# Shared-key attention in half-array tiles with a null column, and a new opening order in the delta rule

## The reference

```
h  = layernorm(x)
q  = h @ Wq                      (16 heads of 64)
kv = h @ Wkv                     (64, keys and values at once)
s  = q . kv / 8, causal;  s_null = q . null / 8
p  = softmax over [s_null, s]
o  = p_null * null + sum_j p_j * kv_j
x += concat(o) @ Wout
```

## Time and profile before

| | us |
|---|---|
| median of 3 runs | 1533.64 (1533.50 to 1539.13) |
| profiled execution | 1534.92 |
| its span | 1533.1 |
| granted TensorE clock, mean | 0.871 |
| first attention, first projection to last add to x | 18.0 to 153.1 |
| opening of the delta rule, first projection to first product of keys | 586.0 to 641.35 |

### The profile page before, as it was taken

How to read it: one execution, slowest core, us unless ns; L and a number is a source line. 1 busy time by engine, 2 the same in 40 slices (tenths; PEclk the granted TensorE clock), 3 DMA queues, 4 the chain that set the end, 5 groups by cost and what they waited for, 6 DMA issues and landing times. The chain is left out here.

```text
span 1533.1 us, 24885 instructions
## 1 busy us (share of the span) xinstructions
PE 1239.6 (81%) x9007; PEld 811.6 (53%) x9008; DVE 892.1 (58%) x2157; ACT 716.1 (47%) x1292; POOL 324.3 (21%) x349
## 2 busy tenths in 40 slices
PE   6999896358697996577776874779789989797998
PEld 3788464237465663235644651765544444364776
DVE  3787473766676546586677568446643455474211
ACT  2444463341274324386568454436566633364432
POOL 0222200003211003454447351021000034300000
PEclk9999798566798997796987897689889999698999
DMA  7000000020000000000000000016045900000000
GB/s 269 1 0 0 1 2 1 0 85 1 1 2 1 1 0 1 0 1 2 1 1 1 1 1 0 2 46 262 2 106 117 211 13 1 0 2 2 1 0 15
DMA packets 15200, 44.28 MB, mean 29 GB/s; under 512 B 1872, under 2 KB 4976, under 8 KB 14448
## 3 DMA queue, kind: packets, MB, share of 16 engines
q1 hardware_dynamic: 15088, 42.80, 9.4%
HBM read 42.01 MB, written 0.79 MB: 28 GB/s over the span
## 5 line engine op out<-in xcount | busy, mean ns | idle before, releaser
L725 DVE TENSOR_REDUCE L_xattn_top<-banks 128x4 f32<-128x512 f32 x128 | 80.7, 672 | 43.9 <-PE banks L585 43.8
L730 DVE TENSOR_TENSOR L_xattn_p<-banks,L_xattn_top 128x512 f32<-128x512 f32 x128 | 82.5, 686 | 4.8
L682 ACT ACTIVATE L_xattn_p<-L_xattn_p 128x512 f32<-128x512 f32 x128 | 75.8, 630 | 18.3 <-DVE L_xattn_p L730 18.2
L690 ACT ACTIVATE L_xattn_pT<-banks 128x512 f32<-128x512 f32 x128 | 69.7, 595 | 19.7 <-PE banks L598 19.7
L585 PE MATMUL banks<-L_xattn_ks,L_xattn_qT 32*128 32x512 f32 x256 | 74.7, 671 | 1.6 <-ACT L_xattn_qT L671 1.6
L598 PE MATMUL banks<-w_const,L_xattn_p 128*128 128x128 f32 x512 | 69.5, 278 | 6.4 <-ACT L_xattn_p L682 6.4
L1252 DVE TENSOR_TENSOR L_ffn_a<-L_ffn_a,L_ffn_share 128x512 f32<-128x512 f32 x64 | 39.9, 686 | 57.6 <-DMA L_ffn_share<-L_ffn_shares 37.0
L1166 PE MATMUL banks<-L_ffn_a,region_a 128*128 128x512 f32 x136 | 67.4, 600 | 4.9 <-DVE L_ffn_a L1252 4.9
L1485 ACT ACTIVATE L_ffn_aT<-banks,L_ffn_shift 128x512 f32<-128x512 f32 x64 | 43.3, 687 | 58.9 <-PE banks L1437 57.3
L1498 DVE SCALAR_TENSOR_TENSOR x<-banks,L_ffn_combine,x 128x128 f32<-128x128 f32 x64 | 18.0, 345 | 88.7 <-PE banks L1448 88.7
L1157 PE MATMUL banks<-hT,region_a 128*128 128x512 f32 x136 | 68.5, 609 | 0.0
(11 more groups left out here) (515 smaller groups left out, 3131.2 us busy)
## 6 DMA issues: line engine op xcount, KB each, us to landing
L_ffn_share<-L_ffn_shares SPq DMA_DIRECT2D x32, 512.0 KB, 9.5
region_b<-in_L_ffn SPq DMA_DIRECT2D x1, 6216.0 KB, 28.9
region_a<-in_L_ffn SPq DMA_DIRECT2D x1, 4416.0 KB, 13.5
region_b<-in_L_attn SPq DMA_DIRECT2D x1, 3150.5 KB, 11.7
region_a<-in_L_ffn SPq DMA_DIRECT2D x1, 3080.5 KB, 21.2
region_b<-in_L_attn SPq DMA_DIRECT2D x1, 1633.5 KB, 9.1
region_b<-in_L_xattn SPq DMA_DIRECT2D x1, 835.0 KB, 9.8
w_tables<-in_tables SPq DMA_DIRECT2D x1, 832.0 KB, 12.8
```

Source lines behind the costliest of these rows:

```text
L682: nc.scalar.activation(p[:, m % 4, :], p[:, m % 4, :], ACT.Exp, scale=scale).then_inc(exped, 1)
L690: nc.scalar.activation(pT[:, n % 2, 2 * (P % 2) + e, :], tps[e][:], ACT.Copy).then_inc(pT_kept, 1)
L725: nc.vector.tensor_reduce(top[:, i, :], rows_of(score[i][:], 4), X, ALU.max)
L730: nc.vector.tensor_tensor(rows_of(p[:, i, :], 4), rows_of(score[i][:], 4), bc(top[:, i, :], 2, T), ALU.subtract).then_inc(centered, 1)
```

## The change

The layer norm of the first attention moves into its block (`NORM_INSIDE`), and the two blocks become one, with the first two units between the projections. Everything is written out, with no loop of the sequencers. The queries stay in two halves of 64 partitions and the keys are held twice, in the upper and the lower half: two heads are scored by products of 64 rows in either half of the array, into two banks. The null key is column 129 of the keys, so a unit's scores are 129 wide (130 with padding), the maximum, the exponential and the sum take it along, and no step of its own is left for it. The exponential reads PSUM and takes the maximum as a bias; its sums come out of the same instruction. GpSimd scales the weights before they are turned. The values have the null vector subtracted, and null @ Wout, the same for every token, is added to x once, at the start. Mixing has the values as weights and gives the outputs already transposed, two heads to the upper and two to the lower half of PSUM, copied by VectorE; the projection follows for two units at once. The copies of the turned weights go to ScalarE and VectorE by turns.

In the delta rule three tiles are projected ahead of `make_rates` and the last ones ahead of the norms of the queries; the two tiles of keys come first; GpSimd takes the taps of tile 2 (values) in place of tile 1, and raises the key norms ahead of squaring the queries' tiles.

```diff
--- before.py
+++ after.py
@@ the old multi_query_attention goes as a whole; a new one stands behind class Norm @@
+def multi_query_attention(nc, g, w, st):
+    NH, DH, Q = 16, 64, 4
+    UNITS = B * NH // Q
+    SCALE = DH ** -0.5
+    W = T + 2
+    norm = Norm(nc, g, st)
+    qT, kvT, kv = st.sb("qT", [128, NH // 2, TOK]), st.sb("kvT", [128, B, W]), st.sb("kv", [T, B, DH])
+    causal, null_wide = st.sb("causal", [T, W], BF16), st.sb("null_wide", [128, T])
+    top, shift, sums, inv = (st.sb(s, [T, 4, Q]) for s in ("top", "shift", "sums", "inv"))
+    p, pT, oT = st.sb("p", [T, 4, Q, W]), st.sb("pT", [T, 3, Q * T]), st.sb("oT", [128, 4, 2 * T])
...
+    tps, oT_bank, out_bank = bank[6], bank[7][:, 0:2 * T], bank[7][:, 2 * T:3 * T]
...
+            nc.gpsimd.memset(causal[:, T:W], 0.0)
+            nc.gpsimd.tensor_copy(causal[:, 0:T], g.causal_bf[:, 0, :]).then_inc(null_ready, 1)
+            pool.wait_ge(w.loaded, 16)
+            nc.gpsimd.tensor_tensor(kvT[:, :, T], bc(w["null2"][:, 0], 1, B), bc(w["null2"][:, 1], 1, B), ALU.add)
+            nc.gpsimd.tensor_tensor(kvT[:, :, T + 1], bc(w["null2"][:, 0], 1, B), bc(w["null2"][:, 1], 1, B), ALU.add)
+            nc.gpsimd.tensor_tensor(null_wide[:], bc(w["null2"][:, 0], 1, T), bc(w["null2"][:, 1], 1, T),
+                                    ALU.add).then_inc(null_ready, 1)
+            norm.invert(pool, 0)
+            norm.invert(pool, 1)
+            for m in range(UNITS):
+                pool.wait_ge(inverted, m + 1)
+                nc.gpsimd.tensor_tensor(p[:, m % 4, :, 0:T], p[:, m % 4, :, 0:T], bc(inv[:, m % 4, :], 2, T),
+                                        ALU.mult).then_inc(normed, 1)
...
+            def make(i, lhsT, half):
+                if i >= 4:
+                    await_kept(pe, i - 4)
+                nc.tensor.matmul(part(i)[:], lhsT, g.hT[:, half * HALF:(half + 1) * HALF], start=True, stop=True).then_inc(made, 1)
...
+                if s >= 3:
+                    pe.wait_ge(exped, s - 2)
+                for a in range(2):
+                    nc.tensor.matmul(bank[k + a][:, 0:2 * W], g.ident_bf[:], bc(causal[:], 1, 2), start=True, stop=False,
+                                     skip_group_check=True)
+                for j in range(2):
+                    for a in range(2):
+                        last = nc.tensor.matmul(bank[k + a][:, j * W:(j + 1) * W],
+                                                qT[64 * a:64 * a + 64, 2 * q + j, n * T:(n + 1) * T],
+                                                kvT[64 * a:64 * a + 64, n, :], start=False, stop=True,
+                                                skip_group_check=True)
+                last.then_inc(scored, 1)
+            def turn(m):
+                pe.wait_ge(normed, m + 1)
+                if m >= 1:
+                    await_pT(pe, m - 1)
+                for i in range(Q):
+                    last = nc.tensor.transpose(tps[:, i * T:(i + 1) * T], p[:, m % 4, i, 0:T], g.ident)
+                last.then_inc(turned, 1)
+            def mix(m):
+                await_pT(pe, m)
+                if m >= 1:
+                    pe.wait_ge(oT_kept, m)
+                if m >= 3:
+                    pe.wait_ge(added, (m - 1) // 2)
+                for a in range(2):
+                    last = nc.tensor.matmul(oT_bank[64 * a:64 * a + 64, :], kv[:, m // 4, :],
+                                            pT[:, m % 3, 2 * a * T:2 * (a + 1) * T], start=True, stop=True)
+                last.then_inc(mixed, 1)
+            def project(h):
+                pe.wait_ge(oT_kept, min(2 * h + 3, UNITS))
+                if h >= 1:
+                    pe.wait_ge(added, h)
+                for m in (2 * h, 2 * h + 1):
+                    for j in range(2):
+                        pair = 2 * (m % 4) + j
+                        last = nc.tensor.matmul(out_bank, oT[:, m % 4, j * T:(j + 1) * T],
+                                                w["wout"][:, pair * D:(pair + 1) * D],
+                                                start=(m % 2 == 0 and j == 0), stop=(m % 2 == 1 and j == 1))
+                last.then_inc(projected, 1)
+            pe.wait_ge(w.loaded, 16)
+            pe.wait_ge(null_ready, 2)
+            for j in range(NH // 2):
+                last = nc.tensor.matmul(bank[0][:, 0:D], null_wide[:], w["wout"][:, j * D:(j + 1) * D],
+                                        start=(j == 0), stop=(j == NH // 2 - 1))
+            last.then_inc(null_done, 1)
+            norm.turn(pe, 0, part(0))
+            pe.wait_ge(kept_act, 1)
+            make(KV0, w["wkv2"], 0)
+            make_queries(Q0[0])
+            norm.turn(pe, 1, part(3))
+            make_queries(Q0[1])
+            make_queries(Q0[2])
+            make_queries(Q0[3])
+            make_values(VAL0, 0)
+            scores(0)
+            make_queries(Q0[4])
+            make_queries(Q0[5])
+            make_queries(Q0[6])
+            scores(1)
+            make_queries(Q0[7])
+            make(KV1, w["wkv2"], 1)
+            for i in Q1:
+                make_queries(i)
+            make_values(VAL1, 1)
+            for s in range(2, UNITS + 6):
+                if s % 2 == 1 and 0 <= s - 7:
+                    project((s - 7) // 2)
+                if s < UNITS:
+                    scores(s)
+                if 0 <= s - 4 < UNITS:
+                    mix(s - 4)
+                if s - 2 < UNITS:
+                    turn(s - 2)
+            def weigh(s):
+                act.wait_ge(shifted, s + 1)
+                if s >= 4:
+                    act.wait_ge(turned, s - 3)
+                k = 2 * (s % 3)
+                for a in range(2):
+                    for j in range(2):
+                        i = 2 * a + j
+                        last = nc.scalar.activation(p[:, s % 4, i, 0:T + 1], bank[k + a][:, j * W:j * W + T + 1], ACT.Exp,
+                                                    bias=shift[:, s % 4, i:i + 1], scale=SCALE,
+                                                    accum_out=sums[:, s % 4, i:i + 1])
+                last.then_inc(exped, 1)
...
+            for s in range(2, UNITS + 2):
+                if s < UNITS:
+                    weigh(s)
+                if s % 2 == 0:
+                    keep_turned(s - 2)
...
+            def keep_values(i, half):
+                dve.wait_ge(made, MADE.index(i) + 1)
+                nc.vector.tensor_tensor(kv[:, 4 * half:4 * half + 4, :], rows_of(part(i)[:, 0:4 * DH], 4),
+                                        bc(w["null_row"][:, 0:DH], 1, 4), ALU.subtract).then_inc(kept_dve, 1)
...
+            def find_shift(s):
+                dve.wait_ge(scored, s + 1)
+                nc.vector.tensor_reduce(top[:, s % 4, :].rearrange("p (a j) -> p a j", a=2), both_banks(s), X, ALU.max)
+                dve.drain()
+                nc.vector.tensor_scalar(shift[:, s % 4, :], top[:, s % 4, :], -SCALE, None, ALU.mult).then_inc(shifted, 1)
+            def invert(m):
+                dve.wait_ge(exped, m + 1)
+                nc.vector.reciprocal(inv[:, m % 4, :], sums[:, m % 4, :]).then_inc(inverted, 1)
...
+            for s in range(2, UNITS + 6):
+                if s % 2 == 1 and 0 <= s - 7:
+                    add((s - 7) // 2)
+                if s % 2 == 0 and 0 <= s - 3 < UNITS:
+                    keep_turned(s - 3)
+                if s < UNITS:
+                    find_shift(s)
+                if 2 <= s - 1 < UNITS:
+                    invert(s - 1)
+                if 0 <= s - 4 < UNITS:
+                    keep_mixed(s - 4)
@@ -2355,10 +2439,10 @@
     NH, DK, DV, TAPS, G, NB = 12, 64, 128, 4, 4, 32
     GROUPS = NH // G
     ORDER = (2, 3, 0, 1, 4, 5, 6, 7)
-    FIRST = (2, 4, 3, 0, 1, 5, 6, 7)
+    FIRST = (2, 3, 4, 0, 1, 5, 6, 7)
     bank, banks = g.bank, g.banks
     TILES = [M for M in range(8 * GROUPS) if M < 8 or M % 8 < 4]
-    pool_tiles = [M for M in TILES if (M == 1 or M >= 8)]
+    pool_tiles = [M for M in TILES if (M == 2 or M >= 8)]
     dve_tiles = [M for M in TILES if M not in pool_tiles]
 
     rate, beta, e, u1, log_u, fix = (st.sb(x, [T, B, NH]) for x in ("rate", "beta", "e", "u1", "log_u", "fix"))
@@ -2536,12 +2620,12 @@
             for i in range(4):
                 last = nc.gpsimd.tensor_copy(pick[:, i, 2 * i:2 * i + 2], g.const["half"])
             last.then_inc(pick_set, 1)
-            add_taps(1)
+            add_taps(2)
             square_tile(0, first_squares(0))
-            square_tile(2, first_squares(1))
-            square_tile(3, first_squares(2))
+            square_tile(1, first_squares(1))
             for part in range(4):
                 key_norms(0, part)
+            square_tile(3, first_squares(2))
             square_tile(4, first_squares(3))
             for hg in range(GROUPS):
                 first, more = B * hg, hg + 1 < GROUPS
@@ -2760,19 +2844,19 @@
             pe.wait_ge(w.loaded, 16)
             project(0)
             project(1)
+            project(2)
```

(39 more changed lines are left out.)

332 lines of the change are left out of this document (128 added, 204 removed).

## The result

The changed kernel takes 1512.07 us (median of 4 runs, 1510.89 to 1513.18), where the kernel before took 1534.45 on the same chip (4 runs, 1533.5 to 1539.13). The ratio is 0.9846, 95% interval 0.9823 to 0.9869: 22.4 us less, where the prediction said 28. The profiled execution of after took 1513.18 us with a span of 1511.4; TensorE's mean granted clock over the span is 0.872, and 0.871 before, so the mean clock isn't behind the gain.

A forecast was written before the change was run, and what follows sets the result against it. A ring between VectorE and TensorE was taken to bound the first attention. Gains of 24 us there and 4 in the delta rule, 28 off 1533.6, gave 1505.6 us; range for 8 in 10: 1493 to 1516.

The forecast's parts named there:

- The ring: First attention: VectorE and TensorE wait on each other in turn, 5.7 us for two units, 2.85 a unit.
- TensorE's own sum: First attention: TensorE's work alone, 2.4 us a unit, or 2.75 if the mixing is serial, against 3.08 before.
- The tenth for a change of form: First attention, TensorE: each switch from one form of tile to another costs 0.1 us, about 0.2 a unit.
- Rival (a): First attention: ring not closed, TensorE bounds at 2.4 us a unit, 1494 us; with dear switches 1509; chance 0.22.
- The first projection: Start of the attention stage: first projection at about 18.2 us, no gain on 18.00 before.
- units 3 to 6: First attention: these units have no projection yet and follow the ScalarE ring, 2.3 us each.
- The tail: End of the attention stage: the last unit falls through the chain in 7.8 us, last addition at 129 us.
- The delta rule: Delta rule's opening: taps out of the way, GpSimd's powers end last, first key matmul at 637.2 for 641.3; gain 4 us.
- rival (e): Delta rule gains nothing because the powers take the place of the taps: +4, 1510 us; inside the forecast's range, no separate chance.
- (c): First attention: tiles of 64 do not run side by side in mixing or scores; 1516 us; chance 0.06.
- (d): First attention: TensorE idles and its clock falls; gain gone from 14 of 32 units, 1568 us with all; chance 0.04.
- (b): First attention: ScalarE's exponentials with sums are dear, 3.0 to 3.2 us a unit, 1513 us; chance 0.15.

The follow-up runs named there:

- the copy on ScalarE: The changed kernel with the copy of the mixed outputs moved from VectorE to ScalarE, TensorE's order untouched: 1511.95 us, ratio 0.9847 to the kernel before.
- the attention-alone run: The changed kernel with the old delta rule put back: 1521.93 us, ratio 0.9880 to the kernel before.
- the delta rule alone: The kernel before with only the new delta rule, its attention as before: 1537.16 us, ratio 0.9991 to the kernel before.
- without sums: The changed kernel with no running sums in the exponentials, the sums set to 1: 1517.22 us, ratio 0.9883 to the kernel before.
- the masks first: The changed kernel with the masks ahead of the projection in TensorE's odd steps: 1510.54 us, ratio 0.9827 to the kernel before.
- the squares first: The changed kernel with GpSimd's two last squarings ahead of its four powers in the delta rule's opening: 1514.98 us, ratio 0.9846 to the kernel before.

## Why the prediction was right, and where it was off

**The ring.** It was right in place, order and size: 5.5 us a pair against 5.7. Its proof is the copy on ScalarE. TensorE's own sum was forecast at 2.4 us a unit and is 2.565: masks to scores 0.31, scores to mixing 0.65, mixing to turning 0.58, turning to masks 0.49, projection 0.53. The tenth for a change of form that was taken from the earlier trace rows fits the masks (two products of 0.11 and 0.1 make 0.31) and falls short at the scores (0.55 forecast, 0.65 measured). Rival (a) named the right second bound with a wrong price: opening the ring gives 5 us in the stage, not 11.

The Trainium skill (TensorEngine Tiling (Array Packing), PSUM Bottleneck) advises both ScalarE and VectorE for emptying PSUM; here moving one of VectorE's two copies gave 0.4 us a pair, so the trace agrees.

**The terms that were mis-sized**, all in the attention, 24 us forecast and 18.8 measured (153.1 to 134.3). The first projection came 1.2 late, because loads ended later in this execution: that of the context, as the first row shows beside the earlier trace rows, and that of the weights, which took 10.8 us where the earlier trace rows has 9.1. GpSimd's operations on the null vector, which read these weights, released the second row.

```profile
9.27 1.94 PE L178 MATMUL banks<-w_const,context_ctx 128*128 128x128 f32 x8 [9.27 <-DMA context_ctx<-in_ctx]
14.12 3.75 PE L409 MATMUL banks<-region_b,L_attn_null_wide 128*128 128x128 f32 x16 [2.92 <-POOL L_attn_null_wide L322]
```

```profile
region_b<-in_L_attn SPq DMA_DIRECT2D x1, 1633.5 KB, 10.8
```

Then 0.6 up to the third unit, and 1.3 in units 3 to 6, 10.3 us for 9. The 25 units after gave 1.2 back (69.8 us for 71). The tail took 11.4 for 7.8, and this 3.6 is the largest miss: I walked one unit through the chain and left out the rounds of earlier units that share bank 7 and VectorE's order with it; banks of their own gave back 2.0 of it. 1.2 + 0.6 + 1.3 - 1.2 + 3.6 = 5.5, the difference to 24 but for rounding.

Only the last two terms are the same in another trace of this attention, that of the attention-alone run. There the first projection starts at 17.9 us, its first four instructions take 1.98 us where after's took 3.76, units 3 to 6 take 9.3, and the last addition ends at 130.1, 1.1 us behind the forecast and not 5.3. So 4.2 us of the attention's miss differ from one execution to the next, with the landing of the loads and TensorE's pace at the start and in units 3 to 6, and a hit or a miss of that size is partly luck.

**The delta rule.** The taps are out of the way and GpSimd's powers, with the squares behind them, come last, as forecast; TensorE's norm products wait for them. After has

```profile
606.08 3.94 DVE L3086 SCALAR_TENSOR_TENSOR region_a<-banks,region_b,region_a 128x1000 f32<-128x1000 f32 x3
```

```profile
606.17 6.45 POOL L2588 TENSOR_TENSOR L_attn_rk<-L_attn_rk,L_attn_power 128x8 f32<-128x8 f32 x4 [10.90 <-DVE L_attn_rk L3117]
612.59 3.74 POOL L2583 TENSOR_TENSOR L_attn_PT<-region_a 128x1024 f32<-128x1024 f32 x2
```

```profile
614.62 1.08 PE L2698 MATMUL banks<-L_attn_PT,L_attn_pick 128*32 128x256 f32 x8 [14.11 <-POOL L_attn_PT L2583]
```

Beside the trace of before that is 5.3 us in the opening and 3.7 in the stage, for a forecast of 4. Beside the old order's other trace it is 1.3 and 0.2, and the timed runs of the delta rule alone hold 0 and 4 us alike. So the order of events was right, but rival (e), no gain, isn't refuted, and that 3.7 lies so near the 4 may be luck. The landmark was badly chosen, too: key matmul and coefficients fell together before, and only the second carries the stage.

**The other rivals.** (c) is out: products on 64 rows or columns run in pairs. (d) is out: the granted clock is 0.98 from 48 to 120 us. (b) is out but for units 3 to 6, where the sums cost 0.7 us in all; the tail without sums took 11.0 us for 11.4.

## What to carry to other kernels

Where two engines hand a pair of steps to and fro, take one instruction off the engine that is not busy and see whether the busy one speeds up: that tells a ring from a full engine, which a reordering on the full one does not, since it changes that engine's own work too. Don't take missing idle time for a wait that is gone: look how closely the instruction follows the one that releases it (0.05 us here, in after and with the masks first). Count the tail of a pipeline bank by bank, with every round that shares one. Choose the landmark whose distance to the stage's end stays nearly constant while the clock does. And set a stage beside more than one trace of the same code before a gain of a few us in it is believed.

## What was not expected of the hardware

Some small operations of VectorE take as long as the squaring that GpSimd is at. Here is the same instruction in after, with GpSimd idle, and in the run with the squares first, where GpSimd squares from 590.9 to 599.1:

```profile
595.41 0.26 DVE L2168 TENSOR_TENSOR L_attn_u<-L_attn_u,L_attn_fix 128x96 f32<-128x96 f32 x1
```

```profile
594.75 1.83 DVE L2168 TENSOR_TENSOR L_attn_u<-L_attn_u,L_attn_fix 128x96 f32<-128x96 f32 x1
...
597.49 1.74 DVE L2172 TENSOR_TENSOR L_attn_e<-L_attn_e,L_attn_log_u 128x96 f32<-128x96 f32 x1
```

Two such cost the earlier squares 3 us of their gain. The Trainium skill (SBUF — State Buffer, SBUF: two separate sides) has VectorE with two inputs in SBUF wait for a whole instruction of GpSimd at a port they share; the 1.8 us beside GpSimd's 1.87 agree.

Each exponential with a sum is two instructions, and the second adds 0.09 us to the pace (0.34 for one in after, 0.25 without sums):

```profile
65.43 0.36 ACT L459 ACTIVATE L_attn_p<-banks,L_attn_shift 128x129 f32<-128x129 f32 x1
65.68 0.20 ACT L459 ACTIVATION_READ_ACCUMULATOR L_attn_p<-banks,L_attn_shift 128x1 f32 x1
```

And the stages behind the first attention, with the same code, took 1376 to 1382 us together in the traces with the new delta rule as it stands in after; the granted clock over these runs was 0.866 to 0.872. That is more than most single edits here are worth, so each edit was read in its own stage.
